# One layer of 44 row tiles in place of sixteen expert passes

## The reference

```python
E, H, I, TOPK = (16, 512, 352, 4)
xs = x[tok]                                    # rows of xn in the order of their experts
gate = jax.lax.ragged_dot(xs, jnp.swapaxes(gate_weight, 1, 2), group_sizes)
up = jax.lax.ragged_dot(xs, jnp.swapaxes(up_weight, 1, 2), group_sizes)
h_act = jax.nn.silu(gate) * up
down = jax.lax.ragged_dot(h_act, jnp.swapaxes(down_weight, 1, 2), group_sizes)
out = jnp.zeros((n_tokens, h), hidden_states.dtype).at[tok].add(down * w_sorted[:, None])
```

## Time and profile before

| | |
|---|---|
| median of 3 runs | 3634.66 us (3632.86 to 3637.85) |
| the profiled execution's own time | 3629.29 us |
| its span in the trace | 3627.7 us |
| granted TensorE clock, mean | 0.995 of full speed |
| `prepare`, from the span's start to the first matmul of `heads` | 475.2 us |
| PE / DVE / ACT / POOL busy, share of the span | 98% / 66% / 64% / 55% |

### The profile page before, as it was taken

The page is one execution under the profiler, slowest core; times in us unless marked ns, Lnnn a source line. Parts: engine busy times, 40 slices in busy tenths (PEclk is TensorE's granted clock), DMA queues, the critical chain, the costliest instruction groups (busy, mean ns, idle before and its releaser), DMA issues. The chain is left out here.

```text
span 3627.7 us, 105696 instructions
## 1 busy us (share of the span) xinstructions
PE 3540.8 (98%) x32416; PEld 2923.7 (81%) x32416; DVE 2393.3 (66%) x5749; ACT 2318.7 (64%) x6430; POOL 1986.7 (55%) x4917
## 2 busy tenths in 40 slices
PE   8999979999999999999999999999999999999999
PEld 6777757888888888888888888888888888877887
DVE  5544446777777777777777777777777777763222
ACT  3444337777777777777777777777777777763111
POOL 3444435666666666666666666666666666653000
PEclk9999989999999999999999999999999999999999
DMA  5543343333333333333443333333333333354543
GB/s 200 203 145 118 133 144 71 75 76 85 76 78 75 81 81 77 76 76 87 114 142 75 83 79 78 75 78 84 76 77 76 83 78 77 98 164 125 142 141 114
DMA packets 420912, 364.13 MB, mean 100 GB/s; under 512 B 190880, under 2 KB 321952, under 8 KB 414496
## 3 DMA queue, kind: packets, MB, share of 16 engines
q1 hardware_dynamic: 418304, 350.90, 35.8%
q0 software_dynamic: 2080, 6.82, 0.5%
HBM read 281.09 MB, written 76.55 MB: 99 GB/s over the span
## 5 line engine op out<-in xcount | busy, mean ns | idle before, releaser
L1254 DVE SCALAR_TENSOR_TENSOR conv<-bank,tap,conv 128x512 f32<-128x512 f32 x1152 | 861.6, 748 | 156.3 <-ACT conv L1390 127.9
L1080 POOL TENSOR_TENSOR prods<-Lb,Tc 128x60 f32<-128x60 f32 (+14 forms) x1920 | 482.2, 251 | 606.7 <-DMA Lb<-base_d 463.4
L1460 PE MATMUL bank<-hx_hi,w_hi 128*128 128x512 f32 x1536 | 663.4, 432 | 0.0
L1460 PE MATMUL bank<-hx_hi,w_lo 128*128 128x512 f32 x1536 | 644.4, 420 | 19.4 <-DVE Tnb L1216 18.1
L1460 PE MATMUL bank<-hx_lo,w_hi 128*128 128x512 f32 x1536 | 637.9, 415 | 0.0
L1087 POOL TENSOR_TENSOR Tc<-Tc,prods 128x56 f32<-128x56 f32 (+13 forms) x1792 | 459.1, 256 | 142.5 <-POOL prods L1080 3.8
L1371 ACT ACTIVATE Wc<-bank 128x128 f32<-128x128 f32 x512 | 141.1, 276 | 366.0 <-PE bank L1562 327.5
L1460 PEld LDWEIGHTS bank<-hx_hi,w_lo 128*128 128x128 f32 x1536 | 292.7, 191 | 58.2 <-DVE Tnb L1216 23.9
L1460 PEld LDWEIGHTS bank<-hx_hi,w_hi 128*128 128x128 f32 x1536 | 292.2, 190 | 36.4
L1208 DVE SCALAR_TENSOR_TENSOR S<-S,gamma,bank 128x128 f32<-128x128 f32 x480 | 167.1, 348 | 228.8 <-PE bank L1573 218.8
L1460 PEld LDWEIGHTS bank<-hx_lo,w_hi 128*128 128x128 f32 x1536 | 292.4, 190 | 29.4
(11 more groups left out here) (198 smaller groups left out, 8979.9 us busy)
## 6 DMA issues: line engine op xcount, KB each, us to landing
Lb<-base_d SPq DMA_DIRECT2D x128, 512.0 KB, 4.7
gamma<-gamma_d SPq DMA_DIRECT2D x128, 258.0 KB, 3.6
alpha<-alpha_d SPq DMA_DIRECT2D x128, 256.0 KB, 3.2
oT_d<-oG SPq DMA_DIRECT2D x128, 256.0 KB, 4.4
gu_raw<-in_gate_up SPq DMA_DIRECT2D x16, 1408.0 KB, 6.4
o_raw<-oT_d SPq DMA_DIRECT2D x13, 1024.0 KB, 6.8
w_raw<-oT_d SPq DMA_DIRECT2D x12, 1024.0 KB, 7.0
hx_hi<-xT_hi_d SPq DMA_DIRECT2D x9, 1024.0 KB, 7.4
```

The source lines that it names most:

```text
L1080: pool.tensor_tensor(prods[:, :, i + 1:], Lb[:, i, :, i + 1:], Tc[:, :, i:i + 1].to_broadcast([P, G, SB - 1 - i]), ALU.mult)\
L1254: dve.scalar_tensor_tensor(out=conv[i][:, to], in0=PJ[PJ_OF[g][i]][:], scalar=tap[:, i, j + 1:j + 2], in1=conv[i][:, to], op0=ALU.mult, op ...
L1460: last = pe.matmul(dst, a[:, i, k], b[:, k], start=(j == 0), stop=(j == 3 * KC - 1))
```

## The change

The 16 x 352 = 5632 inner rows of all experts are taken as one layer of 44 full tiles of 128 rows. A tile may hold rows of two experts. The loop has four rounds of four experts, and 4 x 352 = 11 x 128, so each round has 11 tiles (`ROUND_E`, `ROUND_T`). Weights, products and shares of a tile lie in rings of three slots (`RING`).

In each tile TensorE does 12 matmuls for gate into one bank (`GATE`), 12 for up into another (`UP`), and then the 12 of the down product of the tile before. The four `DOWN` banks are written by all 44 tiles and emptied once, at the end.

Since the banks add up over experts, the share is multiplied in ahead of the down product. There an inner row lies on a partition and a token in a column, so the share is a full tile: the shares are transposed, stored to DRAM (`route_d`, 16 x 512), and for each tile a DMA spreads the row of its expert over the tile's partitions (`rt`). VectorE multiplies Silu(gate) by `rt`, then by up.

The first two tiles' work, the transposes of x and the loads are ordered anew at the start; the gates of group 0 move into tile 4; groups 2r and 2r + 1 belong to round r and start at its tiles 0 and 5; `x_in` is normalised in place; the cuts of Wo stand at tiles 1, 3, 5 and 7 of round 0 and that of the first head's weights at tile 9 (on VectorE; on GpSimd before).

```diff
+ROUND_E, ROUND_T, RING = 4, 11, 3
+EXPERT_AT = {0: 2, 3: 3, 6: 4, 8: 5}
+WO_AT, W_AT = {1: 0, 3: 1, 5: 2, 7: 3}, 9
...
-    DOWN, PREP = (bank[4], bank[5], bank[2], bank[3]), bank[6:8]
+    GATE, UP, DOWN, PREP = bank[0], bank[1], bank[2:6], bank[6:8]
...
+            def load_down(r, u):
+                row = fixed(sp, (r * ROUND_T + u) * P, E * I - P)
+                wait(sp, dn_lo_done, r * ROUND_T + u - back(u) + 1)
+                sp.dma_start(dn_raw[:, slot(u)], down.rearrange("e i n -> (e i) n")[bass.ds(row, P)])\
+                  .then_inc(dn_loaded[slot(u)], 16)
...
+                wait(sp, shared_done, r * ROUND_T + u - back(u) + 1)
+                for e, (q, i0, off, n) in zip(experts, pieces(u)):
+                    sp.dma_start(rt[off:off + n, slot(u)], route_d[bass.ds(e, 1)].to_broadcast([n, GT]))\
+                      .then_inc(rt_loaded[slot(u)], 16)
...
 VectorE:
-                        dve.tensor_tensor(h[0:n, m], gated[0:n, m % 2], bank[2 * (m % 2) + 1][0:n, :], ALU.mult)\
-                           .then_inc(h_done, 1)
...
-                        dve.scalar_tensor_tensor(out=moe[:, t], in0=DOWN[t][:], scalar=route[:, t, bass.ds(e, 1)],
-                                                 in1=moe[:, t], op0=ALU.mult, op1=ALU.add).then_inc(moe_done, 1)
+                    wait(dve, gated_done, t + 1)
+                    wait(dve, rt_loaded[s], loads(r, u, lambda v: len(pieces(v))))
+                    dve.tensor_tensor(h[:, s], h[:, s], rt[:, s], ALU.mult).then_inc(shared_done, 1)
+                    wait(dve, up_done, t + 1)
+                    wait(dve, shared_done, t + 1)
+                    dve.tensor_tensor(h[:, s], h[:, s], UP[:], ALU.mult).then_inc(h_done, 1)
...
 TensorE:
+            def turn(r):
+                for u in range(ROUND_T):
+                    t = r * ROUND_T + u
+                    wait(pe, gu_hi_done, t + 1)
+                    wait(pe, gu_lo_done, t + 1)
+                    wait(pe, gated_done, t)
+                    gate_or_up(r, u, 0, GATE).then_inc(gate_done, 1)
+                    wait(pe, h_done, t)
+                    gate_or_up(r, u, 1, UP).then_inc(up_done, 1)
+                    for g, first in groups(r):
+                        if begun(g) and u in (first + 2, first + 3):
+                            turn_tiles(g, (0, 1) if u == first + 2 else (2, 3))
+                        if u == first + 4:
+                            if isinstance(g, int) and g == 0:
+                                wait(pe, routeT_done, 1)
+                            gates(g)
+                    if u:
+                        add_down(r, u - 1, first=isinstance(r, int) and r == 0 and u == 1)
+                    elif not (isinstance(r, int) and r == 0):
+                        add_down(r - 1, ROUND_T - 1)
+
+            rounds(pe, turn)
+            add_down(FINAL, ROUND_T - 1, final=True)
```

More of the change, by code:

```diff
@@ L334, in _ @@
+            rounds(sp, turn)
             wait(sp, xT_stored, NG * 32)
@@ L400, in _ @@
+            rounds(pool, turn)
         @block.vector
@@ L517, in take, with down_high @@
+            def down_high(r, u):
+                wait(act, dn_loaded[slot(u)], loads(r, u))
+                wait(act, down_done, r * ROUND_T + u - back(u) + 1)
+                act.activation(dn_hi[:, slot(u)], dn_raw[:, slot(u)], ACT.Copy).then_inc(dn_hi_done, 1)
             def take(g, tiles):
@@ L582, in _ @@
+            rounds(act, turn)
+            for i in (0, 2):
+                wait(act, sum_done, i + 1)
+                act.activation(moe[:, i], DOWN[i][:], ACT.Copy)
         @block.tensor
@@ L600, in gates, with gate_or_up, add_down @@
                 last.then_inc(z_done, 1)
+            def gate_or_up(r, u, part, dst):
+                s = slot(u)
+                for k in range(KC):
+                    pe.matmul(dst[:], gu_hi[:, s, k, part], x_hi[:, k], start=(k == 0), stop=False)
+                    pe.matmul(dst[:], gu_hi[:, s, k, part], x_lo[:, k], start=False, stop=False)
+                    last = pe.matmul(dst[:], gu_lo[:, s, k, part], x_hi[:, k], start=False, stop=(k == KC - 1))
+                return last
+            def add_down(r, u, first=False, final=False):
+                t, s = r * ROUND_T + u, slot(u)
+                wait(pe, dn_hi_done, t + 1)
+                wait(pe, dn_lo_done, t + 1)
+                wait(pe, h_hi_done, t + 1)
+                wait(pe, h_lo_done, t + 1)
+                for i in range(TT):
+                    rows = slice(i * P, (i + 1) * P)
+                    pe.matmul(DOWN[i][:], h_hi[:, s, rows], dn_hi[:, s], start=first, stop=False)
+                    pe.matmul(DOWN[i][:], h_hi[:, s, rows], dn_lo[:, s], start=False, stop=False)
+                    last = pe.matmul(DOWN[i][:], h_lo[:, s, rows], dn_hi[:, s], start=False, stop=final)
+                    if final:
+                        last.then_inc(sum_done, 1)
+                if not final:
+                    last.then_inc(down_done, 1)
```

478 lines of the change are left out of this document (229 added, 249 removed).

## The result

The changed kernel takes **3586.44 us** (median of 4 runs, 3584.84 to 3587.96), against 3633.76 for the kernel before, measured beside it (4 runs, 3630.17 to 3637.85): ratio 0.9874, 95% interval [0.9859, 0.9888]. It is 47.3 us faster. The prediction was 3592.0, between 3583 and 3610. The profiled executions took 3629.29 before and 3584.84 after.

A forecast was written before the change was run, and what follows sets the result against it. The prediction took TensorE's dense row of matmuls, busy for 98% of the span, to bound the kernel. Its terms summed to -42.7 us, from 3634.7 to 3592 us, with a range of 3583 to 3610.

The forecast's parts named there:

- Matmuls, -33.1: Expert layer on TensorE: 144 matmuls fewer, 397.1 us becoming 364.0 us, with nowhere to hide.
- Start, -0.4: Layer's opening: first matmul 6.35 us earlier, gates in tile 4 cost +3.7, half-speed opening +2.3; bounds -3 to +3.
- Memset and slow clock, -3.9: Early layer: no clearing of `moe` saves a 2.25 us wait and restart (-2.4), and the slow clock after it (-1.5).
- Additions, -3.0: TensorE's 7 waits for additions into `moe`, 2.4 us in all, go together with their restarts.
- last gates, -4.9: Layer's last gates: idle time before them goes (3.4 us) and they no longer run slowly (1.55 us).
- Chain of a tile, 0: Work behind gate and up products: the added share product costs nothing, with 4.6 us of cover at the tightest.
- The shares' transfers, 0: Loads spreading shares over partitions land in 3.2 us, issued 16.5 us ahead, so they cost nothing.
- Crowded tiles, +2.0: Round 0, tiles 1, 3, 5, 7: VectorE work and transfers make `h` late in tile 5; bounds 0 to +10.
- End, +0.6: Layer's end: the last down product waits for the last tile's `h_lo`, 3.2 us against 2.73 of cover.
- B (feeding): Round 0: transfers and crowded VectorE tiles stop TensorE several times; layer gains only 25 us, 3610; chance 0.12.
- C (chain): Three-slot ring: late shares stretch tiles; at a 10 us period the kernel is slower, 3668 us; chance 0.03.
- D (heads gives back): Layer shortens but `heads` loses 0 to 2 us to last stores, 5 to 10 if unlucky, so 3602; chance 0.06.

The follow-up runs named there:

- kernel 2: The changed kernel with tile 8 of each round issued twice, 144 matmuls more: 3623.37 us, ratio 0.9951.
- kernel 5: The kernel before with 144 matmuls fewer in the layer and nothing else changed: 3616.39 to 3628.16 us, ratio 0.9963.
- kernel 3: The changed kernel with weight rows of gu_hi and gu_lo padded from 128 to 176 numbers: 3598.67 us, ratio 0.9879.
- kernel 7: The changed kernel with 19 idle 128x256 matmuls on the identity ahead of and between the first transposes: 3610.62 us, ratio 0.9941.
- kernel 1: The changed kernel with GpSimd making rstd behind the two low parts of its tile, not ahead of h_lo: 3581.51 us, ratio 0.9842.
- kernel 10: The changed kernel with 19 more matmuls of only 8 columns, all before the first transposes: 3600.91 us, ratio 0.9928.
- Kernel 6: The kernel before with `moe` cleared by GpSimd in place of VectorE: 3634.71 us, ratio 0.9992.
- kernel 4: The changed kernel without the product of Silu(gate) with the shares and without the loads of the shares' tiles: 3607.21 us, ratio 0.9907.
- kernel 12: The changed kernel with the product with the share cut to 8 of 512 columns, loads and instruction counts kept: 3581.04 us, ratio 0.9865.
- kernel 8: The changed kernel with both rstd moved behind the low parts and 19 idle 256-column matmuls at the start: 3612.42 us, ratio 0.9934.
- kernel 11: The changed kernel with rstd moved behind the low parts and 36 idle matmuls of 128 columns at the start: 3592.70 us, ratio 0.989.
- kernel 9: The changed kernel, word for word, measured again (source of the second profile): 3582.28 us, ratio 0.9867.

## Why the prediction was right, and where it wasn't

The forecast held: gain 42.7 predicted, 47.3 measured, 44.5 between the two profiled executions. Two of its own signs of being wrong came all the same: waits of over 0.2 in the steady rounds, and a `heads` longer than 3152 in the first profile (3154.25; 3149.99 in the second). `heads` starts 46.2 us earlier in the first profile and 43.1 in the second; I had 432, and they read 428.95 and 432.11. By its steps:

- *Matmuls, -33.1.* Right in mechanism, shown by kernel 2 (32.3 to 35.4 for 144 added). The test from the other side, kernel 5, gave only 9 to 18 us in the time and has no profile that could say why, so it neither shows nor refutes the term. Missed: the distance itself fell from 0.231 to 0.2267 for gate and up, 1056 x 0.0043 = 4.5 us more. I took the distance as given for 512 columns; it also depends on the layout of the weight tiles (kernel 3). The prediction's test, "not wider than 0.231", was met.
- *Start, -0.4.* The first matmul at 17.89 (18.1 predicted); the opening at half speed costs 5.28 - 2.86 = 2.4, with kernel 7's first twelve for comparison (2.3 predicted). Following the distances of the starts, and not the granted clock, was right: the window of 20 to 22 reads 1.00 after the change too, with matmuls 0.43 apart, and 0.50 in kernel 1 with the same distance. The number of slow ones varies: 12, 8 in the second profile, 14 in kernel 1. Kernel 7 shows that earlier matmuls of 256 columns take this cost away, kernel 10 that matmuls of 8 columns do not.
- *Memset and slow clock, -3.9.* Kernel 6: -4.0 at the start of `heads`.
- *Additions, -3.0; last gates, -4.9.* Their waits are gone from the rows above.
- *Chain of a tile, 0.* The step that failed, in part. The chain's own length was right (kernels 4 and 12: 0.8 us at most for 44 products), but I counted only the instructions of the chain, and not what stands ahead of them in GpSimd's queue. "No wait over 0.2 in the steady rounds" was wrong: 1.12, 1.12 and 1.20 in rounds 1 to 3. Kernel 1 shows the cause and takes it away.
- *The shares' transfers, 0.* The load lands in 7.0 us by the median of the 32 whole tiles, not 3.2, and 16.5 us of lead cover that.
- *Crowded tiles, +2.0.* 0.35 in one execution, 2.94 in the other: inside the bounds. The tile was right and the way only half: it isn't the late `h` that TensorE waits for, but `h_lo` behind `rstd`. Kernel 1 takes this wait away too. The sum also took 397 GB/s for the most that the trace of before shows; a window of it reads 417 (56 to 58), so the crowd of transfers was nearer to nothing than the sum made it. On the two engines: a GpSimd instruction that falls into VectorE's `w_lo` takes 3.12 or 3.34 us, against 1.3 to 1.4 alone, and ends 1.1 us after it. That agrees with the rule of the Trainium skill, "SBUF — State Buffer", section "Who interferes with whom", which the prediction weighed at +5 for this tile; 2.94 lies between the two sums.
- *End, +0.6.* It was 0.20.

The errors nearly add up. First profile: -42.7 - 4.5 (distance) + 4.0 (waits for `h_lo`) - 2.6 (the +2.0 and +0.6 that the sum had for such waits) = -45.8, against -46.2. Second: 2.6 more of such waits, 1.5 of slow clock behind the long one, 0.8 less opening and 0.3 less start: -42.8, against -43.1.

Of the rivals, B (feeding) didn't come: the window of 50 to 100 moved 331 GB/s without TensorE waiting for a transfer, and the wait in round 0 is one for `h_lo`. C (chain) didn't come: `rt` is not in VectorE's list of waits. D (heads gives back) didn't come in this kernel, +1.7 and -2.5 us. But it was priced too low: I gave it up to 10 us, for the last stores and an unlucky start, and otherwise took `heads` as fixed because its instructions are the same. The same instructions took from 3148.5 to 3188.3 in the kernels here. That this change kept the 3152 was luck: my argument could not know it.

What stays open is what sets the length of `heads`. Shown is that instructions added at the front of TensorE's queue, with no effect on the layer, cost 18.6 us and bring waits on `issue` (kernel 10). What the longer executions lost can be read, if not why. All of TensorE's waits between 440 and 3570 add up to 45.2 us in the first profile of after, and to 66.2, 59.3 and 64.8 in kernels 4, 7 and 8; the granted clock of these executions is 0.995, 0.994, 0.993 and 0.992, and 0.001 of it over 3600 us is 3.6 us. By this estimate waits and clock make +24.6, +21.3 and +30.4, where `heads` is longer by 23.1, 21.7 and 34.0. The runs say the same: their mean granted clock is 0.9913 in kernel 7, 0.9905 in 8, 0.9927 in 10 and 0.9930 in 11, and 0.9952 and 0.9945 in the two measurements of after; in kernels 7, 8 and 10 the slowest run has the lowest clock. Whether the waits bring the clock down is not shown. Nor is it shown why kernel 4, with fewer instructions on VectorE and SyncE and the same on TensorE, lost 23 us, why kernel 3, with the same numbers everywhere and only padding between the weights, lost 9, nor which lengths are good.

## What to carry to other kernels

A sum over an in-order queue needs every instruction that stands ahead of the one waited for, on each engine of the chain, and what those wait for; a small one like `rstd` was worth 3 to 6 us. Price matmuls by the distance of their starts, and read that distance again where the layout of the weights changes: it was 0.2267 with tiles at multiples of 512 bytes and 0.232 at multiples of 704. Read an edit in one stage from the time at which the next one starts: the rest of a long program can get 20 us and more longer although the edit doesn't touch it. Its waits and its granted clock say where that time went.

## What the runs showed of the hardware

- The distance of fp32r matmuls of 512 columns is 0.2267 us with weight tiles at multiples of 512 bytes (after the change) and 0.232 at multiples of 704 (kernel 3).
- The granted clock of a window can read 1.00 or 0.50 while TensorE's first matmuls run at half speed; fifteen matmuls of 256 columns on the identity ahead of the transposes (5.1 us), and four more in the gaps behind, take that away (kernel 7: 2.9 us for 12 matmuls in place of 5.3). Nineteen of 8 columns, 6.8 us long, do not (kernel 10).
- A GpSimd `tensor_tensor` of 128x512 takes 1.3 to 1.4 us alone and 3.12 beside a VectorE `tensor_tensor` of 128x2048 that began 0.29 us earlier; it ends 1.12 us after it (kernel 9).
- 19 matmuls of 8 columns in an idle stretch made the kernel 18.6 us slower and its runs scatter over 28 us, where those of the same kernel without them lie within 4 (kernels 10 and 9).
